# Edge attention on a graph: how the edges ahead of each node are counted in the first stage

## What is computed

```python
q, k, v = layer_norm(x @ Wq), layer_norm(x @ Wk), layer_norm(x @ Wv)
ke, ve  = layer_norm(edge_attr @ Wke), layer_norm(edge_attr @ Wve)
rel_k = layer_norm(concat(ke, k[src]) @ relk_W + relk_b)
qk    = sum(q[dst] * rel_k) / 4
lse   = segment_logsumexp(qk, dst)
rel_v = layer_norm(concat(ve, v[src]) @ relv_W + relv_b)
h     = (qk - lse[dst]) * rel_v
agg   = segment_sum(h, dst)
out   = layernorm(x + layer_norm(relu(agg @ z_W + z_b)))
```

## Time and profile before

| | |
|---|---|
| median of 3 runs | 3041.61 us (3037.26 to 3042.23) |
| the profiled execution, own time | 3035.95 us |
| its span, first to last instruction | 3034.2 us |
| busy in the span: PE, DVE, ACT, POOL | 94%, 96%, 76%, 80% |
| counts in it: L626, L627, L628 | 13 of each, from 45.6 to 112.4 us |
| start of the edge stage on GpSimd | 193.8 us |

### The profile page before, as it was taken

One profiled execution on the slowest core, in us unless ns is written; L12 is line 12 of the kernel. 1 busy time (PEld: TensorE's weight loads), 2 busy tenths in 40 slices (PEclk: granted clock), 3 DMA queues, 4 the chain that ended last, 5 costly groups with the idle time before them and its releaser, 6 DMA issues. The chain is left out here.

```text
span 3034.2 us, 76084 instructions
## 1 busy us (share of the span) xinstructions
PE 2840.4 (94%) x18870; PEld 2515.5 (83%) x18870; DVE 2907.3 (96%) x3387; ACT 2306.6 (76%) x5276; POOL 2414.6 (80%) x2622
## 2 busy tenths in 40 slices
PE   4659999999999999999999999999999999997954
PEld 3349999999999999999999999999999999995633
DVE  7879999999999999999999999999999999997947
ACT  2448888888888888888888888888888888885526
POOL 7768888888888888888888888888888888883773
PEclk9889999999999999999999999999999999998977
DMA  3468888888888888888888888888888888886642
GB/s 88 148 188 244 259 255 258 254 257 256 256 258 254 259 256 255 256 256 257 256 256 257 255 257 255 257 254 258 256 255 255 256 257 254 258 263 209 162 122 77
DMA packets 660921, 715.95 MB, mean 236 GB/s; under 512 B 97993, under 2 KB 554430, under 8 KB 660469
## 3 DMA queue, kind: packets, MB, share of 16 engines
q1 hardware_dynamic: 568201, 499.33, 52.4%
q0 software_dynamic: 84896, 211.42, 27.1%
q10 hardware_dynamic: 7756, 4.43, 0.6%
HBM read 482.62 MB, written 231.46 MB: 235 GB/s over the span
## 5 line engine op out<-in xcount | busy, mean ns | idle before, releaser
L1312 POOL DMA_INDIRECT e_rows<-node_table,e_gcol x1564 | 1932.7, 1236 | 422.6 <-issue 306.0
L1132 PE MATMUL banks<-w_edge,e_eat 128*128 128x240 f32 x6256 | 1396.3, 366 | 0.7 <-ACT e_ysq L1241 0.7
L1132 PEld LDWEIGHTS banks<-w_edge,e_eat 128*128 128x128 f32 x6256 | 1188.7, 190 | 89.5 <-issue 1.1
L1125 PE MATMUL banks<-e_h,e_oh 128*128 128x248 f32 x3128 | 805.2, 380 | 3.8 <-DVE e_h L1427 3.6
L1422 DVE TENSOR_REDUCE e_zs<-e_z 128x96 f32<-128x1440 f32 x391 | 638.9, 1634 | 0.2
L1125 PEld LDWEIGHTS banks<-e_h,e_oh 128*128 128x128 f32 x3128 | 534.1, 191 | 37.0 <-DVE e_h L1427 6.4
L1211 ACT ACTIVATE e_agg<-banks 128x496 f32<-128x496 f32 x782 | 453.8, 580 | 90.0 <-PE banks L1125 89.7
L1220 ACT ACTIVATE e_oht<-banks 128x512 bf16<-128x512 f32 x391 | 233.4, 597 | 313.2 <-PE banks L1145 310.8
L1410 DVE TENSOR_TENSOR e_p<-banks,e_yr 128x960 f32<-128x960 f32 x391 | 447.0, 1143 | 4.8 <-PE banks L1132 3.5
L1390 DVE TENSOR_TENSOR e_p<-e_p,e_rows 128x960 f32<-128x960 f32 x391 | 447.0, 1143 | 0.0
L1427 DVE TENSOR_TENSOR e_h<-e_p,e_zw 128x960 f32<-128x960 f32 x391 | 445.8, 1140 | 1.2 <-POOL e_zw L1325 1.2
(11 more groups left out here) (413 smaller groups left out, 2656.4 us busy)
## 6 DMA issues: line engine op xcount, KB each, us to landing
tile_sums<-e_agg SPq DMA_DIRECT2D x391, 496.0 KB
e_q<-q_by_rank SPq DMA_DIRECT2D x1564, 96.0 KB
e_ea<-in_edge_attr SPq DMA_DIRECT2D x390, 256.0 KB
e_rows<-node_table,e_gcol POOLq DMA_INDIRECT x1564
edge_lse<-t_lse_sb SPq DMA_DIRECT2D x14, 448.0 KB, 3.6
edge_qk<-e_qkt SPq DMA_DIRECT2D x130, 48.0 KB
node_table<-n_tb SPq DMA_DIRECT2D x24, 240.0 KB, 2.8
n_x<-in_x SPq DMA_DIRECT2D x24, 128.0 KB, 2.3
```

What stands on the lines that cost most here:

```text
L1125: last = nc.tensor.matmul(sums_bank(x, loop, half)[:, (j % 2) * AW:(j % 2 + 1) * AW], oh[:, x % OR, j, :], hh[:, x % HR, j, :, :].rearrang ...
L1132: last = nc.tensor.matmul(out_ps[:, j // 2, (j % 2) * 2 * HC:(j % 2 + 1) * 2 * HC], eat[:, x % 4, j * P:(j + 1) * P], t["w_edge"][:, at:at ...
L1312: g.indirect_dma_start(out=rows[:, k, j, :], out_offset=None, in_=table, in_offset=bass.IndirectOffsetOnAxis(ap=gcol[:, kb, at:at + 1].bit ...
```

## The change

In `count(k)` the comparison over four blocks (L626) and the sum over each of them (L628) are gone. The copy to `w_of` now comes first, without a link, and counts up a semaphore of its own (`s_wof`), for which `sum_rows` waits. Then follows one `tensor_scalar` for each block: it compares the 128 values with the node's number, which is now a scalar of each partition, adds 0.0, and gives out the sum of its 128 results to `cnt` besides the results themselves (`accum_out`). No wait stands between the four. That makes 49 such instructions, and 13 comparisons and 13 sums less.

```diff
@@ -275,6 +275,7 @@
     s_hit = [sem(f"tile_dst_gathered{i}") for i in range(SETS)]
     s_cnt, s_lb, s_lbn, s_here, s_pre, s_idx = (sem("edges_counted"), sem("first_edges_ready"), sem("next_edges"), sem("nodes_present"),
                                                 sem("present_summed"), sem("rank_rows_ready"))
+    s_wof = sem("first_rank_of_tile")
     s_nrow, s_nf = sem("rank_code_rows"), sem("rank_code_loaded")
     s_f0, s_sqr, s_f1, s_f2, s_fresh = (sem("feature_rank"), sem("rank_squared"), sem("feature_high"), sem("feature_low"), sem("flags_ready"))
     s_ro, s_rst, s_ri, s_key, s_kst, s_ki = (sem("first_ranks_int"), sem("first_ranks_stored"), sem("first_ranks_loaded"), sem("keys_ready"),
@@ -623,9 +624,12 @@
                 dve.wait_ge(s_hit[k], 16 * nb)
                 if k >= 1:
                     dve.wait_ge(s_cnt, k)
-                link(v.tensor_tensor(out=cmp4[:, 0:nb, :], in0=hits[:, bs, 0:P], in1=n_f[:, bs].unsqueeze(2).to_broadcast([P, nb, P]), op=ALU.is_lt))
-                link(v.tensor_copy(out=w_of[:, bs], in_=hits[:, bs, P]))
-                v.tensor_reduce(out=cnt[:, bs], in_=cmp4[:, 0:nb, :], axis=AX.X, op=ALU.add).then_inc(s_cnt, 1)
+                v.tensor_copy(out=w_of[:, bs], in_=hits[:, bs, P]).then_inc(s_wof, 1)
+                for i in range(nb):
+                    b = SLOTS * k + i
+                    last = v.tensor_scalar(out=cmp4[:, i, :], in0=hits[:, b, 0:P], scalar1=n_f[:, b:b + 1], scalar2=0.0, op0=ALU.is_lt, op1=ALU.add,
+                                           accum_out=cnt[:, b:b + 1])
+                last.then_inc(s_cnt, 1)
 
             def rank_rows():
                 dve.wait_ge(s_cnt, SETS)
@@ -644,6 +648,7 @@
                 v.tensor_tensor(out=row_idx[:], in0=wk[:, 1, :], in1=pre[:], op=ALU.add).then_inc(s_idx, 1)
 
             def sum_rows():
+                dve.wait_ge(s_wof, SETS)
                 link(v.tensor_tensor(out=t["degree"][:], in0=lb_next[:], in1=lb[:, 0:BLOCKS], op=ALU.subtract))
                 link(v.tensor_scalar(out=t["end_pos"][:], in0=lb_next[:], scalar1=-1.0, scalar2=0.0, op0=ALU.add, op1=ALU.max))
                 link(v.tensor_scalar(out=j_i[:], in0=t_i[:], scalar1=TILES - 1, scalar2=None, op0=ALU.bitwise_and))
```

## The result

The changed kernel took 3034.98 us (median of 18 runs, 3030.62 to 3037.08) against 3040.2 us for the kernel before, run beside it (18 runs, 3035.91 to 3042.85): a ratio of 0.9985, interval 0.9979 to 0.9991. It is 2.7 to 6.4 us faster. The forecast was 3042.3 us, 0.7 us slower, with 3037.5 as the lower end of its range: the sign and the range were both wrong, though the change does stay within 0.2%.

A forecast was written before the change was run, and what follows sets the result against it. VectorE's counts in the first stage, up to first_pos, were taken as the path that starts the edge stage. With first_pos 0.7 us later, 3041.61 + 0.7 = 3042.3 us; range 3037.5 to 3047.5 us.

The forecast's parts named there:

- The bound: First stage, VectorE's counts: shorter ones give back at most 1.01 us a round, longer ones cost in full.
- one of the signs of being wrong: VectorE's copy in the counts: the prediction would be wrong if it stalled for GpSimd's gathers too.
- the pitch p: Start to start of the new TENSOR_SCALARs in a count: taken as 0.42 us, bounded by 0.21 and 0.56 us.
- The term of 0.15 us for giving out the sum: New instruction in the counts: giving out its row sum costs up to one more smallest instruction, 0.15 us (L549).
- its low end: Lower bound for the new instruction's start-to-start time in the counts: 0.21 us, with the sum for free.
- the cheaper 0.29 us row: L1370, a 128x128 TENSOR_SCALAR of 0.29 us, against 0.35 us for L604; it leaves about 0.21 us start to start.
- the cheap rival: Counts at 0.21 to 0.25 us an instruction: first_pos near 109.8 us, 2.9 us earlier, 3038.7 us; chance 0.11.
- C: VectorE's cost of a full set's count: 0.09 us copy plus four new instructions, 1.77 us against 1.52.
- What first_pos gains, the kernel gains: Round 12 to the edge stage: what first_pos (L632, 112.72 us) loses or gains, the kernel loses or gains.
- the forecast loss: End of round 12: first_pos starts at 113.45 us instead of 112.72, making the kernel 0.7 us slower.

The follow-up runs named there:

- the repeat: The changed kernel run once more without an edit, against the kernel before: 3034.72 us, ratio 0.9985.
- the copied-first kernel: The kernel before with the copy to w_of first and unlinked in each count, comparison and sum kept: 3038.16 us, ratio 0.9995.

## Why the prediction was wrong

- **The bound was right upwards, and only in part downwards.** The sets' counts are on the path, set 1 isn't, and a shift of the first stage goes through the edge stage unchanged (3.0 us at its start, 2.9 at its end). But shorter counts run into the gathers, in sets 6 and 7: one of the signs of being wrong that the prediction named. The price of a shorter count, where no gather holds VectorE up, does go through (4.42 us a round for 4.86).
- **The step that failed is the pitch p.** The forecast took p = 0.35 + 0.15 - 0.08 = 0.42 us. The main part's share, 0.35 - 0.08 = 0.27, was right to 0.01 us. The term of 0.15 us for giving out the sum was wrong: the readout is there, 0.08 us long, but beside the next main part, so the term is 0. The text granted an overlap to the tail of a result, named full overlap of the sum for its low end alone, and there joined it to the cheaper 0.29 us row. The value that rows and overlap give together, 0.27, stood in the text as a part of the sum and belonged to no case: the forecast began at 0.36 and the cheap rival ended at 0.25. C was 1.77 us and measures 1.13.
- **The Trainium skill was nearer, in part by luck.** "VectorE: DVE Perf Modes" gave an estimate of 0.254 us a pitch; the rows have 0.265 to 0.267. Its two instructions are the two rows. But the estimate's 0.194 us for the main part and 0.060 for the second are not what the rows show, which is 0.265 and nothing. The prediction set it aside because L604's row reads 0.35 us. A row's duration isn't a pitch, though: the new instruction's successor starts 0.08 us before the row ends.
- **The cheap rival had the right kind of path, and its number by luck.** It had the gathers hold VectorE up, the copy stand for the first memset, and first_pos near 109.8 us: measured 109.90. But VectorE reached set 11 at 107.27 us, not at 103.6, with no gather to wait for there. The memset ended at 109.20 instead of 108.33, and the four came through with the copy instead of behind it: two errors of 0.9 us that cancel. In the repeat no copy stood at all. Its price, 2.9 us, is near what the profiles differ by (2.82 at first_pos, 3.17 at the stage's end). It got a chance of 0.11.
- **What is queued behind a stalled instruction isn't added to the stall.** For the copy moved ahead the prediction added the comparison behind the memset's end; both the copied-first kernel (111.63 us for both) and the changed one (109.23 for all five) show them end together.
- **"What first_pos gains, the kernel gains"** holds only roughly. Of L637's stall 0.47 us of 1.9 lay on the path; the node table's store, TensorE's slow stretches and the landing of the last scatter add or take back up to 3 us.
- **The level.** The forecast started from the median of three runs, 3041.61 us. More runs of before, the two slow chips aside, have medians of 3038.8 to 3040.2 us. Of the 7.3 us by which the forecast missed, 1.4 are this, 0.7 the forecast loss, and 5.2 the gain.
- **Open.** The two timings of the changed kernel lie 5.2 and 4.1 us under before; the profiles show 3.2 and 2.4 us at the stage's end. The timings' intervals reach down to 2.7 and 1.8 us, so the 2.4 to 3.2 us may be all. Of anything more, shorter waits for the node table's store (1.22 and 3.40 us after, 1.64 and 3.49 before) are half a microsecond that is already in the 3.2. Whether the shifted rounds also meet fewer slow stretches of TensorE wasn't settled: no kernel here fixes where these fall. Nor do the runs split the gain for good between the sets ahead of round 12 and round 12 itself: the two profiles of the changed kernel gain, counted from the first gather, 1.9 and 0.8 us up to set 11, and 1.2 and 2.1 us in round 12.

## What to carry to other kernels

Price an instruction by the distance from its start to the next start, not by its row's duration, and carry that through for every part of it, a readout too. Where two unlinked instructions stand back to back, take the overlap as the likeliest case, and give a chance to each value that the rows allow, without a gap between the cases. Before a stall is counted as gained or lost, look at what the next instruction waits for once it is gone, and don't add to it what is queued behind it without a wait.

## What the runs showed of the hardware that I had not expected

- A comparison with a row sum, 128x128 fp32, has a pitch of 0.27 us unlinked, 0.39 linked; without the sum 0.19. The readout of the sum, 0.08 us, runs beside the next instruction: another comparison, a plain one (61.62 us) or a TENSOR_TENSOR (58.59 us).
- While a GpSimd memset runs, the form with the sum goes through in 0.35 us, if nothing that stands is ahead of it. A plain TENSOR_SCALAR and a 128x4 copy stand until the memset ends: up to 2.7 and 2.6 us in these runs, and 3.6 for a plain one that started beside the gather just ahead. Unlinked instructions behind a standing one start at their usual pitch and end with it.
- A GpSimd memset of 128x3072 started right behind the last indirect scatter lengthens its landing from 4.5 to 6.65 us, in three executions of three; one of 5x3072 there costs next to nothing (4.5 us in both executions that have it).
